# Moving one of the two q, k, v projection tiles of a batch to the slot of the output projection

## The reference

```python
h = _layernorm(x) * (1 + ca) + sa                # per batch modulation
xn = rms_norm(h, ln1_w)
q, k, v = (xn @ Wq), (xn @ Wk), (xn @ Wv)        # each 256 x 128 per batch
q, k = normalize_kq(q), normalize_kq(k)          # per head, by the root of the sum of squares
attn = (einsum('bqhd,bkhd->bhqk', q, k) + bias) * scale
attn = softmax(where(causal, attn, -1e6))
y = einsum('bhqk,bkhd->bqhd', attn, v) @ Wo + h
```

## Time and profile before

| | us |
|---|---|
| three runs | 730.47, 735.51, 730.84 |
| median | 730.84 |
| profiled execution, its own time | 729.48 |
| its span, first to last instruction | 727.0 |
| busy in the span: TensorE, VectorE | 489.9, 442.6 |
| busy in the span: GpSimd, ScalarE | 420.3, 278.1 |
| mean granted TensorE clock | 0.865 |

### The profile page before, as it was taken

The page is one execution under the profiler, slowest core; times in us unless marked ns, Lnnn a source line. Parts: engine busy times, 40 slices in busy tenths (PEclk is TensorE's granted clock), DMA queues, the critical chain, the costliest instruction groups (busy, mean ns, idle before and its releaser), DMA issues.

```text
span 727.0 us, 15153 instructions
## 1 busy us (share of the span) xinstructions
PE 489.9 (67%) x4424; PEld 381.2 (52%) x4425; DVE 442.6 (61%) x1317; ACT 278.1 (38%) x579; POOL 420.3 (58%) x636
## 2 busy tenths in 40 slices
PE   2568888888887767766666623168768767667157
PEld 0335555555555555655445522067767766567136
DVE  5876888888888754777787787035344343433127
ACT  0256777877877634332433322012222222112000
POOL 5565666666665000477766777607777777677710
PEclk9868999999999999787788755579998899989569
DMA  7993000000060050011111111135334443341178
GB/s 217 293 263 104 0 0 1 0 0 0 0 232 4 1 174 1 28 59 50 57 53 53 54 57 58 57 103 139 104 103 119 115 114 102 98 120 52 51 282 310
DMA packets 65243, 65.94 MB, mean 91 GB/s; under 512 B 8896, under 2 KB 56224, under 8 KB 65200
## 3 DMA queue, kind: packets, MB, share of 16 engines
q1 hardware_dynamic: 47472, 41.28, 19.5%
q0 software_dynamic: 9216, 19.94, 8.1%
q10 hardware_dynamic: 8512, 4.20, 2.0%
HBM read 40.86 MB, written 27.67 MB: 94 GB/s over the span
## 4 chain that ended last, share of the span: by engine, by line
issue 25%; POOL 22%; DVE 20%; PE 19%; ACT 6%; DMA 4%; DVEq 2%; POOLq 1%; SPq 1%; ACTq 0%
POOL ys L630 16%; DVE L L1238 6%; PE PS L996 4%; POOL xs L617 4%; PE PS L881 2%; PE PS L1155 2%; PE PS L1008 2%; POOL QKR L515 1%; ACT YT L684 1%; PE PS L1019 1%; PE PS L856 1%; DMA srep<-in_scale 1%; PE PS L904 1%; PE PS L884 1%; DVE XH L1201 1%
## 5 line engine op out<-in xcount | busy, mean ns | idle before, releaser
L617 POOL DMA_INDIRECT xs<-QKT,posi x128 | 124.8, 975 | 109.3 <-issue 98.3
L1238 DVE TENSOR_TENSOR L<-PS,BIAS 128x768 f32<-128x768 f32 x128 | 116.6, 953 | 39.4 <-PE PS L884 33.7
L677 ACT ACTIVATE PR<-L 128x768 f32<-128x768 f32 x128 | 105.9, 842 | 60.9 <-DVE L L1238 58.7
L630 POOL DMA_INDIRECT ys<-hid,yidx x80 | 76.6, 958 | 45.7 <-issue 25.6
L1086 PE MATMUL PS<-BIAS,V 128*128 x320 | 68.0, 361 | 49.1 <-DVE V L1594 48.8
L630 POOL DMA_INDIRECT ys<-YT,yidx x80 | 76.6, 957 | 24.4 <-issue 23.2
L1086 PEld LDWEIGHTS PS<-BIAS,V 128*128 128x128 f32 x320 | 56.2, 205 | 55.5 <-issue 55.5
L791 ACT ACTIVATE L<-PS 128x384 f32<-128x384 f32 x40 | 19.6, 491 | 162.4 <-PE PS L1086 162.4
L881 PE MATMUL PS<-QKT 32*128 32x256 f32 x512 | 47.3, 439 | 27.2 <-DVE L L1238 25.7
L996 PE MATMUL PS<-YT,w1s 128*128 128x256 f32 x128 | 42.2, 487 | 15.8 <-ACT YT L741 15.8
L1608 DVE TENSOR_TENSOR hid<-PS,tag 128x512 f32<-128x512 f32 x20 | 13.8, 692 | 60.1 <-DMA ys<-hid,yidx 60.1
(11 more groups left out here) (247 smaller groups left out, 1121.4 us busy)
## 6 DMA issues: line engine op xcount, KB each, us to landing
PR<-xs SPq DMA_DIRECT2D x160, 72.0 KB
BIAS<-ys SPq DMA_DIRECT2D x12, 512.0 KB, 7.8
modb<-mod_rows SPq DMA_DIRECT2D x1, 4096.0 KB, 14.3
dist_rep<-dist_row SPq DMA_DIRECT2D x4, 768.0 KB, 7.1
xs<-pad_row SPq DMA_DIRECT2D x1, 2376.0 KB, 19.3
X<-in_x ACTq DMA_DIRECT2D x4, 512.0 KB, 6.9
BIAS<-dist_rep SPq DMA_DIRECT2D x4, 512.0 KB, 9.0
xs<-QKT,posi POOLq DMA_INDIRECT x128, 2.3
```

What stands on the lines that cost most here:

```text
L617: pool.indirect_dma_start(out=xs, out_offset=bass.IndirectOffsetOnAxis(ap=posi[j][:, t * TOPK + k:t * TOPK + k + 1], axis=0), in_=ROWS[j][ ...
L630: pool.indirect_dma_start(out=ys, out_offset=bass.IndirectOffsetOnAxis(ap=yidx[par][:, j:j + 1], axis=0), in_=yo[par][:, j * P:(j + 1) * P ...
L677: act.activation(PR[u % 4][:, :], L[u % 2][:, :], ACT.Exp).then_inc(s["exp_done"], 1)
L1238: return dve.tensor_tensor(L[u % 2][:, :].rearrange("p (j w) -> p j w", j=2), PS[:, at:at + 2, 0:HW], BIAS[:, u, :].rearrange("p (j w) -> ...
```

## The change

`qkv` gets a list of tiles. Tile 0 of batch b+3 is projected in turn b, behind `y_out(b-1)` and ahead of `pair(b+1, 0)`; tile 1 stays where both were, in turn b+1. The waits stand ahead of tile 0, and `qkv_done` is raised behind tile 1. Batches 0 to 2 are projected whole as before (batch 2 in turn 0), batches 3 to 15 in two halves.

```diff
-            def qkv(b, par):
-                pe.wait_ge(s["hT_ready"], b + 1)
-                if at(b, 1):
-                    pe.wait_ge(s["raw_done"], 1)
-                elif not at(b, 0):
-                    pe.wait_ge(s["qkt_act"], b - 1)
-                    pe.wait_ge(s["qkt_dve"], b - 1)
-                for t in range(TPB):
+            def qkv(b, par, tiles=range(TPB)):
+                if 0 in tiles:
+                    pe.wait_ge(s["hT_ready"], b + 1)
+                    if at(b, 1):
+                        pe.wait_ge(s["raw_done"], 1)
+                    elif not at(b, 0):
+                        pe.wait_ge(s["qkt_act"], b - 1)
+                        pe.wait_ge(s["qkt_dve"], b - 1)
+                for t in tiles:
                     last = pe.matmul(bank(PRE + t, 3 * D), hT[par][:, t * P:(t + 1) * P], wqkv[:, :], start=True, stop=True)
-                last.then_inc(s["qkv_done"], 1)
+                if TPB - 1 in tiles:
+                    last.then_inc(s["qkv_done"], 1)
...
                 if left >= 2:
-                    qkv(b + 2, par)
+                    qkv(b + 2, par, range(TPB) if first else [1])
                 pair(b, par, 1)
...
                 if not first:
                     y_out(b - 1)
+                if left >= 3:
+                    qkv(b + 3, 1 - par, [0])
                 if left >= 1:
                     pair(b + 1, 1 - par, 0)
                 products(b, par, 2)
```

## The result

The changed kernel takes 751.31 us (median of 4 runs, 749.16 to 755.85) beside 733.17 us for the kernel before (4 runs, 730.47 to 736.19); the ratio is 1.0254, interval 1.0182 to 1.0327. It is slower, as forecast, but beyond the range's upper end of 748.0. Once more beside 23 runs of the kernel before (median 730.63) it took 749.74, ratio 1.0254 (1.0221 to 1.0288).

What follows compares the result with a forecast made beforehand. Attention was taken as a ring of TensorE's scores and VectorE's additions; batches of 14.52 instead of 13.54 us and +1.0 at batch 0 to 1 gave +12.7, so 743.5 us, range 739 to 748.

Steps and rivals of the forecast that it cites:

- Where the wait ends: TensorE, done with y_out, stands 1.57 us ahead of tile 0, until ScalarE's squares raise hT_ready; start 0.06 later.
- Tile 0: Projection of one tile in the new slot behind y_out: 0.75 us, half of two, or up to 0.82.
- Add 0 to add 2: VectorE's additions of scores and bias: with a tile removed, this step becomes 3.19 us everywhere, VectorE's own pace.
- GpSimd's squares late in each batch: VectorE's 0.28 us wait for GpSimd's squares would be seen each time, making add 2 to add 4 3.36 us.
- Batch 0 to 1: The 13th place of the change, at half clock: +1.0 us, from bounds 0.8 and 1.2.
- Sum at full clock: Whole kernel: 12 batches of 14.52 instead of 13.54 us, 11.7 longer, and +1.0 for batch 0 to 1: +12.7 us.
- granted clock 1.00 through the loop: Sign expected in the new profile: TensorE keeps 2.4 GHz through attention's loop; a fall would make the prediction wrong.
- the second rival: TensorE's idle time in each batch lets its clock fall: about 779 us, or 755 in a third of batches; chance 0.07.
- The rival's price: Clock rival's cost at half clock, start of pair(1, 0) to add 2: 7.91 against 5.17 us, 2.7 a batch.
- First rival: Wait hidden: hT_ready in time, tile 0 fills TensorE's idle 0.69 us before the next scores; about 728 us, chance 0.05.

Runs made afterwards that it cites:

- The wait alone: Kernel before, with only the new wait for hT_ready ahead of pair(b+1, 0), both tiles in the old slot: 748.39 us, ratio 1.0222.
- the work alone: Changed kernel whose tile 0 in the new slot reads the hT of the batch before, so it has no new wait: 727.73 us, ratio 0.9957.
- filler: Changed kernel with the output projection's two matmuls done three times over ahead of the wait, same result: 744.53 us, again 744.49 us.

## Why the prediction was wrong, point by point

- Where the wait ends: right. TensorE idle 1.55 us (1.57 was worked out), released by the squares, start 0.06 behind them. The wait alone costs 18 us by the medians and 15.3 by attention (with its own cold batches), the work alone nothing.
- Tile 0: taken as half of two, 0.75, with 0.82 as its upper bound; it takes 0.84 alone in its slot. This is the 0.09 by which a batch is 14.61 and not 14.52.
- Add 0 to add 2 at VectorE's pace of 3.19, and GpSimd's squares late in each batch: right (3.18, and 3.36 for add 2 to add 4 in the batches whose clock stays up).
- Batch 0 to 1: +1.0 was taken from rows at half clock. From add 6 of batch 0 (51.35 and 51.51) to add 2 of batch 1 (61.57 and 61.39) it is 10.22 against 9.88, +0.3; in the repeated profile it is 10.89, +1.0. The clock comes back in this stretch at a different moment in each profile, so its share can't be fixed closer.
- Sum at full clock: +12.7 forecast, +13.3 and +14.1 in the two profiles with filler (228.72 and 229.49 less 215.40), +13.9 by the medians. This mechanism and its size were right.
- The step that failed is the clock. The sum holds no term for it ("granted clock 1.00 through the loop"), and the second rival, which names it, was given 0.07 on the strength of one row, the wait of 1.54 us in batch 15 that passed at full clock. That row says what happened once, at a place that comes once. The change put a wait of that length into each of 13 batches, and in five or six of them the clock fell. On the chip of the repeated run the loss of 19.1 us is 13.9 at full clock, against 12.7 forecast, and 5.2 for the clock, against nothing. The Trainium skill's "TensorE: Matmul & The Clock Gate", section "A second HAM failure mode: psum-queue depth-cycling", which had been named against the change, describes this in another kernel: frequent small gaps between groups of matmuls make the gate go down and up. The runs agree with it, in 5 or 6 of 12 batches at a gap of 1.55, in 4 of 12 at 1.63 with one tile less work in the slot, and in none at 0.97 and 0.66.
- The rival's price was off the other way: 2.7 us a batch had been taken from batch 0, where products and projection ran at half clock too. In batches 3, 5 and 7 the clock is back about when the products begin (L906 at 164.43 with 0.70), and only tile 0 and the scores are slow: 16.07 - 14.61 = 1.46. In 8, 10 and 12, where the clock falls later, scores and products are slow, and a batch takes up to 16.19. Six times 1.46 are 8.8 us, and the profile's attention is 237.20 - 228.72 = 8.5 longer than with filler.
- The range left this out, because the clock was priced only at 2.7 us a batch, in every batch (779) or in a third of them (755). The shares that the profiles show (4 to 6 of 12) are not far from that third; the price was too high. At the measured 1.46, six cold batches on top of 743.5 give 752, beside the measured 751.31.
- First rival: its condition was the one given, ScalarE makes hT ahead of exp 6. Where hT is there in time the kernel takes 727.73 and 728.34 us, where 728 had been worked out. That they agree so closely is partly luck: as gains they are 2.2 and 1.6 us on a chip where the kernel before takes 729.96, and 2.9 had been worked out from 730.84.
- One reading at the start was a little off without entering the sum: attention's last additions are at 257 us, in the 15th slice, and some 470 us come behind it, not 465.

## What to carry to other kernels

Work moved into an engine's idle time takes its waits along; look first when its last input is ready there, and what else its semaphore stands for. Here the idle 0.69 us was real and the tile fitted, but its input was 1.6 us late, 0.6 of that for squares that it doesn't read. Moving the producer ahead of one instruction, with a semaphore of its own, turned 2.5% of loss into a small gain. And where a change adds an idle time of TensorE to every turn of a loop, a single wait of that length which passed at full clock says little: reckon with some turns at half clock, and test it with filler work.

## What the runs showed of the hardware

TensorE's granted clock fell from 2.4 to 1.2 GHz in a loop in which it was busy 11.9 of 14.6 us, with no idle time longer than 1.55 us; with 0.98 or less at the same place it stayed up throughout the loop. The fall can come at the end of the idle time (tile 0 at 1.65 instead of 0.91) or a little behind the work that follows it (products at 1.08 behind scores at 0.71 in the kernel with the wait alone).

The falls are not scattered as if by chance. With the wait alone the cold batches are 3, 6, 9 and 12, exactly every third. In the changed kernel they are 3, 5, 7, 8, 10 and 12 in one profile and 3, 6, 8, 10 and 12 in the other, mostly every second. What sets this distance was not tested.

VectorE's x_hat took 0.92 us instead of 0.65 for the same two operations when a GpSimd operation on 128 x 256 elements began 0.15 us ahead of them; the first of the two ended 0.08 us behind it.
